# Two attention layers with gated experts: where the value products stand among the key-major score tiles of a step

## The reference

```python
energy = jnp.einsum('bhqd,bhkd->bhqk', q, k)          # layer 0: + a clipped relative bias per head
att = jax.nn.softmax(energy / (scaling * temp), axis=-1)   # layer 1: causal mask instead of the bias
out = jnp.einsum('bhqk,bhkd->bhqd', att, v)
```

## Time and profile before

| | us |
|---|---|
| median of 3 runs | 1306.81 |
| lowest and highest run | 1296.58, 1309.57 |
| the profiled execution | 1299.84 |
| its span | 1297.9 |
| attention of layer 0, first to last exponential | 268 to 657 |
| attention of layer 1, first to last exponential | 741 to 1026 |

### The profile page before, as it was taken

One profiled execution on the slowest core, in us unless ns is written; L12 is line 12 of the kernel. 1 busy time (PEld: TensorE's weight loads), 2 busy tenths in 40 slices (PEclk: granted clock), 3 DMA queues, 4 the chain that ended last, 5 costly groups with the idle time before them and its releaser, 6 DMA issues.

```text
span 1297.9 us, 18539 instructions
## 1 busy us (share of the span) xinstructions
PE 1126.3 (87%) x6826; PEld 526.3 (41%) x6826; DVE 808.7 (62%) x1582; ACT 649.2 (50%) x1246; POOL 193.0 (15%) x309
## 2 busy tenths in 40 slices
PE   5599999799899999999875792899999799897777
PEld 3366666222222322322123341434443367643344
DVE  6633333789598899887038581878785235465554
ACT  4332322157587777778524251656777522334344
POOL 2145653000010010010100000102231000001000
PEclk9699999679799999999677575979999899999888
DMA  4521224132101101100004432111023310000331
GB/s 140 180 84 50 89 89 88 49 76 70 45 23 35 35 19 35 43 11 18 10 10 127 146 65 68 44 35 36 29 89 107 105 56 1 1 1 1 131 131 33
DMA packets 62165, 77.93 MB, mean 60 GB/s; under 512 B 15760, under 2 KB 39936, under 8 KB 60032
## 3 DMA queue, kind: packets, MB, share of 16 engines
q1 hardware_dynamic: 62080, 76.81, 19.5%
HBM read 61.58 MB, written 14.56 MB: 59 GB/s over the span
## 4 chain that ended last, share of the span: by engine, by line
PE 68%; DVE 13%; SPq 6%; DMA 5%; ACT 5%; issue 2%; POOL 0%; DVEq 0%; ACTq 0%
PE PS L1496 66%; DVE mx L1289 5%; ACT arena L883 4%; SPq L532 3%; DMA sums<-arena 2%; DMA arena<-k_dram 1%; SPq L539 1%; SPq L550 1%; DVE arena L1470 1%; PE PS L1509 1%; DMA arena<-drev_dram 1%; DVE arena L1103 1%; DVE arena L1106 0%; DMA arena<-mrow 0%; DVE small L1456 0%
## 5 line engine op out<-in xcount | busy, mean ns | idle before, releaser
L1496 PE MATMUL PS<-arena 128*32 128x512 f32 (+13 forms) x3656 | 621.1, 491 | 72.6 <-DVE mx L1289 38.7
L883 ACT ACTIVATE arena<-PS 128x512 f32<-128x512 f32 (+3 forms) x896 | 438.7, 557 | 270.0 <-PE PS L1496 266.1
L1289 DVE TENSOR_REDUCE mx<-PS 128x1 f32<-128x512 f32 (+3 forms) x896 | 506.8, 625 | 103.0 <-PE PS L1496 99.1
L1496 PEld LDWEIGHTS PS<-arena 128*32 128x32 f32 (+3 forms) x3656 | 159.3, 105 | 444.5 <-DVE mx L1289 178.7
L1496 PE MATMUL PS<-x_hi,w_hi_lo 128*128 128x512 f32 x320 | 144.9, 495 | 1.2 <-DVE fw L1390 0.8
L1390 DVE TENSOR_TENSOR fw<-PS,fw 128x512 f32<-128x512 f32 x80 | 55.3, 692 | 119.7 <-ACT fw L930 117.9
L930 ACT ACTIVATE fw<-PS 128x512 f32<-128x512 f32 x80 | 47.8, 597 | 123.5 <-PE PS L1496 123.5
L821 POOL TENSOR_TENSOR fw<-fw,arena 128x512 f32<-128x512 f32 x64 | 84.9, 1327 | 88.9 <-DVE fw L1390 88.9
L1496 PE MATMUL PS<-fw 128*128 128x512 f32 (+3 forms) x184 | 90.3, 578 | 0.0
L774 POOL TENSOR_TENSOR arena<-arena,fw 128x512 f32<-128x512 f32 x32 | 41.0, 1281 | 265.5 <-DMA fw<-sum_dram 265.5
L1496 PEld LDWEIGHTS PS<-x_hi,w_hi_lo 128*128 128x128 f32 x320 | 61.0, 191 | 31.2 <-issue 19.5
(11 more groups left out here) (281 smaller groups left out, 1030.2 us busy)
## 6 DMA issues: line engine op xcount, KB each, us to landing
arena<-comb_dram SPq DMA_DIRECT2D x16, 1024.0 KB, 5.2
fw<-sum_dram SPq DMA_DIRECT2D x32, 256.0 KB
arena<-comb_dram SPq DMA_DIRECT2D x16, 512.0 KB, 7.3
arena<-k_dram SPq DMA_DIRECT2D x16, 408.0 KB
q_dram<-arena SPq DMA_DIRECT2D x24, 256.0 KB, 3.7
k_dram<-arena SPq DMA_DIRECT2D x24, 256.0 KB, 3.8
arena<-q_dram SPq DMA_DIRECT2D x16, 384.0 KB
arena<-drev_dram SPq DMA_DIRECT2D x32, 192.0 KB, 3.6
```

The source lines that it names most:

```text
L883: s.activation(Pr[:, m % 8, 0:w], bank(4 + m % 3, 0, w), ACT.Exp).then_inc(A["e_done"], 1)
L1289: v.reduce_max(mx[:, H % 2, kh, n:n + 1], bank(U % RING, 0, w), axis=AX.X, negate=True).then_inc(A["ring_free"], 1)
L1496: return nc.tensor.matmul(out_, lhsT, rhs, start=start, stop=stop)
```

## The change: what it does

In both layers, `av_step` of the step before is issued behind tile 1 and no longer behind tile 2. The units of a quarter still follow. No instruction is added or removed, and no wait is changed; the order of TensorE's instructions in a step goes from

```diff
@@ -1656,7 +1656,7 @@
                         n = len(todo)
                         for j in range(HG):
                             st_step(H, i, j)
-                            if j == 2 and before:
+                            if j == 1 and before:
                                 av_step(*before)
                             for what in todo[n * j // HG:n * (j + 1) // HG]:
                                 ring_unit(what)
```

## The result

The changed kernel takes 1333.17 us (median of 4 runs, 1331.17 to 1336.52) against 1308.19 for the kernel before (4 runs, 1296.58 to 1313.80): a ratio of 1.0208, 95% interval 1.0158 to 1.0258. The change makes it slower by about 2%. The profiled execution took 1333.20, its span is 1331.3.

What follows compares the result with a forecast made beforehand. A ring of waits through ScalarE and TensorE was taken to bound the kernel. Layer 0's +18.8 and layer 1's +3.6 gave +22.4 us, put on 1303.2 for 1326; range 1311 to 1339.

Steps and rivals of the forecast that it cites:

- the mechanism: Common layer 0 steps: tile 2 comes behind the products, tile 3 follows at exponential spacing; 2.60 against 2.43, +.17.
- layer 1's halves 0 to 13: Narrow steps about even; +.5 a pair over six pairs, the first pair left out before a longer wait.
- even 1 (behind the copy): Step 1 of an even half in layer 0: products wait for the copy, tile 3 at 468.43 against 467.95, +.48.
- The ring: Layer 0 steps: waits through ScalarE and TensorE, from one tile 3 exponential to the next, make the 2.43 us period.
- half 14: Layer 0: unit behind tile 1 in tile 2's rows; five steps of 2.80 for 2.40, plus step 1: +2.7.
- The .20 of a unit in tile 2's rows: A unit sharing rows with the tile behind it costs .20; about 30 places, bounds 0 to .20.
- No starvation of VectorE: VectorE waits for the moved unit behind tile 1, with about 12% idle to cover it.
- item 4: Layer 0, even step 5 to odd step 0: products start .62 early, the M unit's wait hides behind them; -.40.
- step 5: Step 5 of the odd half in layer 0: its M wait hides behind the products, 0.
- the sum has no clock term: TensorE's clock: half 14 and the end of layer 1 keep 2.4 GHz, so no clock loss was added.
- rival 3: Longer TensorE pauses drop the clock, sixteen steps at half clock cost 17 us on top: 1343; chance .06.
- The base: The +22.4 was put on 1303.2, the mean of all four known executions of the kernel before.

Runs made afterwards that it cites:

- `four_banks`: Kernel before with four banks for the tiles and three for the units, products still behind tile 2: 1308.76 us, ratio 1.0003.
- `tail_banks`: Kernel before with three banks for units and four for tiles from half 14, all seven for tiles where no units are left: 1293.74 us, ratio 0.9969.
- `layer0_only`: New order in layer 0 alone, layer 1 with the order of the kernel before: 1330.57 us, ratio 1.0231 to the kernel before.
- `before_filled`: Kernel before with one unread extra matmul per step in tail halves and 18 in the pause before layer 0's half 15: 1301.76 us, ratio 1.0053.
- `behind_fourth`: Kernel before with the value products moved from behind tile 2 to behind tile 3: 1318.67 us, ratio 1.0050.
- `after_filled`: Changed kernel with two unread extra matmuls per step in tail halves and 18 before layer 0's half 15: 1336.80 us, ratio 1.0319 to the kernel before.
- `tail_filled`: `tail_banks` plus the filling, six banks for tiles and products behind tile 3 where no units are left: 1284.75 us, ratio 0.9908 to the kernel before.

## Why the prediction was right, and where it was off

The time, 1333.2, lies in the range 1311 to 1339, 7 above the forecast of 1326, and in layer 0 the mechanism was the named one. That the total fits so well is in part luck: the two first profiles differ by 33.4 us and not by 22.4, because of the clock (below), and the forecast had been put on a base 3.4 above the profiled execution. By stretch, layer 0's halves 0 to 14 gave +21.4 for the +18.8 forecast, and layer 1's halves 0 to 13 +.9 for +3.0: two misses that nearly cancel. In the steps that the prediction worked out, the distance from tile 3's exponential to the next one changed by (halves 8 and 9, read from both traces):

| steps | forecast | measured |
|---|---|---|
| 0 of the even half, 4, 6, 7 of the odd one | +.17 each | +.17 each |
| even 1 (behind the copy) | +.48 | +.47 |
| even 2 | +.19 | +.17 |
| even 3 and 4 | +.59 | +.56 |
| even 5 to odd 0 | -.40 | -.19 |
| odd 1, 2, 3 | +.29, +.27, +.49 | +.27, +.28, +.49 |
| odd 5 | 0 | +.11 |
| a pair | +2.6 | +2.84 |

**Right, shown by runs.** The ring: cut by a fourth bank, half 14's step fell from 2.40 to 2.07. Tile 2's place and not its bank: 2.78 with four banks too. The .20 of a unit in tile 2's rows: .22 with the unit moved. No starvation of VectorE: 2.60 with the unit in front. That `av_done` and the other queues cost nothing was argued and not tested by a run.

**Off in size: item 4 and step 5.** The prediction let the M unit's wait for the ring vanish behind the products. Part of it came back one place earlier. In step 5 the unit behind tile 0 now waits for VectorE, and with it tile 1 and the products:

```profile
483.98 0.11 PEld L1496 LDWEIGHTS PS<-arena 48*128 48x128 bf16 x2 [0.62 <-DVE mx L1289]
...
484.52 0.16 PEld L1496 LDWEIGHTS PS<-arena 128*32 128x32 f32 x8 [0.43 <-ACT arena L883]
```

The products start at 484.52; tile 3's exponential ended at 484.36, so .16 late instead of .05. That gives +.11 for the step in each half. Item 4 came out at -.19 instead of -.40 and step 5 of the odd half at +.11 instead of 0, together .32 a pair; this wait is .22 of it, 1.1 us over halves 4 to 13. The other .10 was not traced.

**Off in size: half 14.** It grew by 3.5 and not by 2.7. From its first to its last exponential it grew by 2.4. The other 1.2 lie between its last exponential and the first one of half 15 (5.1 us before, 6.3 after). The last row-maximum unit now stands behind the products. Its reduction, from which GpSimd's casts, the M unit and the transfer for half 15 follow, starts 1.2 us ahead of half 14's last exponential (639.02 and 640.22), where it started 2.2 ahead (620.06 and 622.26), and the M unit now waits for the casts:

```profile
641.10 0.24 PE L1496 MATMUL PS<-identb,mparts 128*48 128x128 bf16 x1 [0.92 <-POOL mparts L768]
```

**Off: "the sum has no clock term".** This is the step that failed. It read from the earlier trace rows that the end of layer 1 keeps full clock at 85% busy and took that for the changed kernel too. The changed kernel spent 35.6 us there instead of 26.1 in both profiles, at .62. That is rival 3, in a place where it had not been looked for, and 9.5 us against the .6 forecast. Of the products' new order in layer 1 the runs show: in all six profiles that had it the clock was down for 27 us or more of this stretch (35.6 to 39.0 us long). In six profiles with the products behind tile 2 there, it was not down at all twice, for 3.4 us twice (`four_banks`, `tail_banks`), and for 10 and 14 us in `layer0_only` and `before_filled`. With the products behind tile 3 (`behind_fourth`) it was down for nearly the whole stretch too. So leaving the old place makes the fall likely, and chance has a share. Why is open: filling part of TensorE's pauses did not prevent it. The Trainium skill ("TensorE: Matmul & The Clock Gate", "A second HAM failure mode: psum-queue depth-cycling") says that micro-idle times between groups of matmuls can make the clock swing, and the prediction had set it aside. The trace has one fall here, from 1022.4 to 1049.7 in the first profile, with no pause of TensorE over .79 us in the 10 us before it. The kernel before pauses for .3 to .5 us in most steps of the same stretch and kept 1.00. Whether the micro-idle times are the cause of the fall no run shows.

**The base.** The profiled execution of the kernel before, 1299.84, was a fast one: its median over later runs is 1307 to 1311. The forecast added to a mean of 1303.2. The two profiles of the changed kernel stand 30 to 47 us above the two of the kernel before, the medians 20 to 25: a common execution of the kernel before has more time at the lower clock (granted .88 to .89 in those of 1305 to 1315 us) than its two profiles (.898 and .912). Layer 1's halves 0 to 13 gave +.9 and not +3.0. In halves 8 to 13, at 1.00 in both kernels, it was +2.5 against the 1.5 forecast for three pairs (+.6, +.6 and +1.3). In halves 0 to 7 the clock differs from profile to profile, as `layer0_only` shows, and the forecast of +1.5 for them is neither borne out nor refuted.

## What to carry to other kernels

When two things wait for the same event, the short one that feeds the engine with least in hand goes first; putting the long one first costs what the consumer then has to do in sequence (two exponentials' spacing, .49) minus the short one's own slot (.32). Follow one step of the ring in the timeline and add it up before trusting busy shares: a ring shows as small idle times on every engine and is cut by one more buffer, but only where the buffer taken from elsewhere is not missed. A profile is one draw: the second one of the kernel before showed that half 15 alone makes 9 us of spread.

## What the runs showed of the hardware

- The granted clock did not follow TensorE's busy share: in `after_filled` it was .59 over 5.2 us in which TensorE was busy throughout with extra matmuls of 48 rows, and in the kernel before it was 1.00 at 22.1 busy of 26.1 us.
- The lower clock lengthened a step without units from 2.39 to 3.69 with three banks for the tiles, and from 2.07 to 3.16 with seven.
- With nothing to wait for, ScalarE's exponentials of 128x512 follow each other at .48 on average (1.91 for four, `tail_filled`). Their recorded lengths there grow from .60 to .94 over half 15, so a recorded length is not what an exponential costs.
